# A graph kernel on one Trainium2 core: when the messages are turned, the rows normed, the nodes loaded and the results stored

## The chip, the cores and the metric

One NeuronCore of a Trainium2 chip runs the whole program; nothing is shared with other cores. The metric is the device time of one execution in microseconds (us), lower is better. TensorE is called PE here, its weight loads PEld, VectorE DVE, ScalarE ACT, GpSimd POOL, and SyncE SP. SP computes nothing here: its queue holds DMA issues. ACT issues DMAs too, in order with its own computing instructions.

## What is computed

There are 4096 nodes with 128 features each, and a 4096 x 4096 matrix `adj` (64 MB in fp32).

```python
h = jnp.maximum(_layernorm(x, axis=-1), 0.0)
x = x + _L0_gnn_ref(h, adj)          # (adj.T @ h) / column sums of adj
h = jnp.maximum(_layernorm(x, axis=-1), 0.0)
x = x + _L1_gnn_ref(h, adj, L1_gnn_W, L1_gnn_b)
# inside _L1_gnn_ref
neigh1 = adj @ x
x1 = jax.nn.swish(neigh1 @ W + b)
neigh2 = adj @ x1
x2 = jax.nn.swish(neigh2 @ W + b)
```

So the matrix is passed over three times: once with its columns as outputs (sweep 1), and twice with its rows as outputs (`adj @ x` and `adj @ x1`, sweeps 2 and 3).

## The kernel before, in words

**Two ways to multiply.** PE multiplies a tile of `adj` with a tile of features either whole, in fp32 (each such matmul shows as two MATMUL records), or split: ACT rounds the tile of `adj` to fp32r (`a_hi`, in sweeps 2 and 3 `at_hi`), POOL subtracts that from the original (`a_lo`, `at_lo`), and PE does three cheaper matmuls, hi x hi, hi x lo and lo x hi. A whole one takes more of PE, a split one takes ACT and POOL. Tables (`WHOLE1`, `WHOLE1_FIRST`, `WHOLE3`) say which tiles are whole.

**Sweep 1.** Output columns go in 4 quarters of 1024 columns. In a quarter there are 16 pairs of row tiles, k = 0 to 15; v = 16 * quarter + k counts all 64. Pair v is one 1 MB load by SP into one of 5 slots of `raw1` (`load1`). SP reuses the slot of pair v - 5 when DVE has added that pair to the column sums (`add_degrees`, L559) and PE and POOL are done with it. PE adds the pair into `m_ps`: whole pairs at L277, split pairs at L282 and L283, with the a_lo part (L295) one pair later. In the first quarter pairs 6, 8, 9, 11, 12 and 14 are split, in the others nine of sixteen.

**The start.** `x` is loaded into `h` in three blocks (tiles 0 to 3, 4 to 15, 16 to 31), DVE takes statistics, POOL makes scale and shift (`norm`), and ACT applies them with Relu (L409, one instruction per tile of 128 x 128). For the nine pairs in `SPLIT_ROWS` it does it twice, into `h_hi` and into `h`; POOL then makes `h_lo` of them (L692). ACT goes through all 32 tiles before its first `a_hi`, that of pair 6. Pairs 2, 3 and 5 are whole in the first quarter and split later, so their `h_hi` is first read in the second quarter.

**Messages of a quarter.** When a quarter's 16 pairs are done, ACT copies `m_ps` to `msgT`. While the next quarter runs, PE turns it: after pair k = 2 `turn_message(q, 0)`, the column sums (L322) and four transposes (L330), and after pair k = 6 `turn_message(q, 1)`, the other four transposes, which wait for `inv_ready`. That comes from DVE's `invert` (L571 to L574, after `add_degrees` of k = 7). DVE adds the two halves of the messages to the nodes `x` at k = 8 and k = 11 (`add_message`) and takes statistics at k = 9 and 12 (`node_statistics`). The nodes come in 16 loads of 128 KB each on SP's queue (L252), one after each pair from v = 5 to v = 20; all must be there for the first `add_message`. Each has 1024 runs of 512 bytes.

**Sweeps 2 and 3.** `adj` is loaded again in pieces of 2 MB (`load3`, L217): two DMAs of 512 KB on SP's queue and two on ACT's. Four slots `raw3` hold pieces. DVE transposes each piece in four units (L602) into a ring of five, `turned`. 256 units in 64 pieces are worked off; every third unit is whole (L351) and the others are split (ACT L455, POOL L715, PE L357, L358, L368). Four pieces of sweep 2 are kept for sweep 3. ACT issues its half of piece i between two of its roundings. After 512 rows ACT copies the sums (L463), after 1024 rows PE multiplies by W (`xw`, L376), DVE adds the bias (L612) and ACT applies Silu (L468); in sweep 3 DVE then adds the nodes (L620) and ACT issues the four stores of 128 KB (`store`, L483). There are four such groups in sweep 3, r = 4 to 7, and the last ends the program.

**Order.** There is no scheduler. Each engine's program is written out by hand, and each engine and queue works strictly in its order; semaphores (`wait_ge`) join them.

## Time and profile before

| | us |
|---|---|
| median of 3 runs | 687.6 |
| lowest and highest | 684.11, 690.33 |
| the profiled execution's own time | 688.42 |
| its span, first to last instruction | 686.6 |

| engine | busy us | share of the span |
|---|---|---|
| PE | 634.4 | 92% |
| POOL | 571.2 | 83% |
| DVE | 523.1 | 76% |
| PEld | 404.0 | 59% |
| ACT | 301.4 | 44% |

The DMA engines moved 199.80 MB, 291 GB/s over the span. How to read it: an engine with 92% can still lose time only where it stands idle, and the 52 us in which PE does are spread over a few places. So the places count, not the shares. The profile also gives the granted clock of PE in each stretch, as a share of 2.4 GHz; half of it is 1.2 GHz.

### The profile page before, as it was taken

How to read it: one execution, taken by the hardware profiler on the slowest of the kernel's cores; microseconds unless marked ns; L12 is line 12 of the kernel's file. 1: busy time of each engine (PE TensorE's matmuls, PEld its weight loads, DVE VectorE, ACT ScalarE, POOL GpSimd, SP SyncE). 2: the span in 40 equal slices, each digit the busy share in tenths (PEclk: the TensorE clock that was granted, in tenths of full speed). 3: DMA queues.
4: the chain of work that ended last, by engine and by line, in shares of the span. 5: the costliest groups of instructions: out<-in, count | busy, mean ns of one | idle time of the engine just before them, and what ended most of it. 6: DMA issues, size and time to landing. Idle time of an engine off the chain costs nothing.

```text
span 686.6 us, 6755 instructions
## 1 busy us (share of the span) xinstructions
PE 634.4 (92%) x2212; PEld 404.0 (59%) x2212; DVE 523.1 (76%) x516; ACT 301.4 (44%) x378; POOL 571.2 (83%) x287
## 2 busy tenths in 40 slices
PE   4888978999998988899999999999999999799994
PEld 2355545666665645556666666667666557466553
DVE  3965789979978839777787777878778778577871
ACT  1943243264272343646445445445444434245250
POOL 2288488689788857998999999999999789599693
PEclk9989999999999998999999999999999999899998
DMA  8999996989999899999999999919999999999941
GB/s 277 352 303 306 298 366 246 329 300 333 329 292 309 286 233 250 345 345 317 328 345 330 329 345 317 279 25 195 327 345 345 315 328 332 305 252 347 311 94 31
DMA packets 155762, 199.80 MB, mean 291 GB/s; under 512 B 5456, under 2 KB 138832, under 8 KB 155728
## 3 DMA queue, kind: packets, MB, share of 16 engines
q1 hardware_dynamic: 86672, 133.18, 62.5%
q10 hardware_dynamic: 69056, 66.20, 35.0%
q8 instruction: 17, 0.28, 0.2%
q14 instruction: 17, 0.14, 0.1%
HBM read 197.26 MB, written 2.10 MB: 290 GB/s over the span
## 4 chain that ended last, share of the span: by engine, by line
PE 55%; POOL 20%; issue 12%; DMA 4%; ACT 3%; DVE 3%; ACTq 1%; SPq 1%; POOLq 0%
PE dg L351 20%; POOL a_lo L701 11%; PE dg L368 9%; PE dg L357 9%; PE dg L358 9%; POOL at_lo L715 7%; PE m_ps L277 4%; DMA raw<-in_adj_dram 2%; PE m_ps L376 2%; DMA h<-in_x_dram 2%; POOL norm L684 1%; PE m_ps L295 1%; PE m_ps L282 1%; PE m_ps L283 1%; ACTq L217 1%
## 5 line engine op out<-in xcount | busy, mean ns | idle before, releaser
L715 POOL TENSOR_TENSOR at_lo<-turned,at_hi 128x1024 fp32r<-128x1024 f32 x160 | 379.8, 2414 | 33.1 <-ACT at_hi L455 28.3
L602 DVE STREAM_TRANSPOSE turned<-raw 128x1024 f32<-128x1024 f32 x256 | 304.1, 1224 | 95.7 <-PE dg L351 41.9
L455 ACT ACTIVATE at_hi<-turned 128x1024 fp32r<-128x1024 f32 x160 | 167.3, 1057 | 208.8 <-DVE turned L602 122.2
L701 POOL TENSOR_TENSOR a_lo<-raw,a_hi 128x1024 fp32r<-128x1024 f32 x66 | 155.1, 2387 | 46.7 <-ACT a_hi L425 44.7
L351 PE MATMUL dg<-turned,f_w 128*128 128x512 f32 x384 | 182.4, 597 | 1.3 <-issue 1.3
L559 DVE TENSOR_TENSOR dg<-raw,dg 128x2048 f32<-128x2048 f32 x60 | 137.5, 2291 | 35.5 <-DMA raw<-in_adj_dram 33.6
L357 PE MATMUL dg<-at_hi,f_hi 128*128 128x512 f32 x320 | 134.9, 422 | 11.5 <-ACT at_hi L455 11.5
L368 PE MATMUL dg<-at_lo,f_hi 128*128 128x512 f32 x320 | 130.9, 490 | 3.1 <-POOL at_lo L715 3.1
L358 PE MATMUL dg<-at_hi,f_lo 128*128 128x512 f32 x320 | 128.4, 401 | 0.0
L277 PE MATMUL m_ps<-raw,h 128*128 128x512 f32 x248 | 116.6, 617 | 11.1 <-DMA raw<-in_adj_dram 11.1
L351 PEld LDWEIGHTS dg<-turned,f_w 128*128 128x128 f32 x384 | 73.2, 191 | 57.0 <-issue 48.5
L425 ACT ACTIVATE a_hi<-raw 128x1024 fp32r<-128x1024 f32 x66 | 66.3, 1051 | 91.1 <-DMA raw<-in_adj_dram 86.0
L368 PEld LDWEIGHTS dg<-at_lo,f_hi 128*128 128x128 f32 x320 | 59.6, 192 | 54.3 <-issue 30.4
L277 PEld LDWEIGHTS m_ps<-raw,h 128*128 128x128 f32 x248 | 48.8, 199 | 63.3 <-issue 57.3
L357 PEld LDWEIGHTS dg<-at_hi,f_hi 128*128 128x128 f32 x320 | 61.3, 192 | 32.8 <-ACT at_hi L455 14.3
L358 PEld LDWEIGHTS dg<-at_hi,f_lo 128*128 128x128 f32 x320 | 61.4, 192 | 16.1 <-issue 2.9
L282 PE MATMUL m_ps<-a_hi,h_hi 128*128 128x512 f32 x132 | 55.1, 417 | 6.3 <-ACT a_hi L425 3.8
L283 PE MATMUL m_ps<-a_hi,h_lo 128*128 128x512 f32 x132 | 53.2, 403 | 0.0
L295 PE MATMUL m_ps<-a_lo,h_hi 128*128 128x512 f32 x132 | 46.1, 466 | 0.0
L282 PEld LDWEIGHTS m_ps<-a_hi,h_hi 128*128 128x128 f32 x132 | 25.6, 194 | 16.2 <-issue 8.8
L295 PEld LDWEIGHTS m_ps<-a_lo,h_hi 128*128 128x128 f32 x132 | 25.4, 192 | 15.0 <-issue 9.1
L283 PEld LDWEIGHTS m_ps<-a_hi,h_lo 128*128 128x128 f32 x132 | 25.8, 195 | 5.4 <-issue 0.5
(47 smaller groups left out, 258.8 us busy)
## 6 DMA issues: line engine op xcount, KB each, us to landing
raw<-in_adj_dram SPq DMA_DIRECT2D x64, 1024.0 KB, 8.9
raw<-in_adj_dram ACTq DMA_DIRECT2D x122, 512.0 KB, 13.5
raw<-in_adj_dram SPq DMA_DIRECT2D x118, 512.0 KB, 11.7
x<-in_x_dram SPq DMA_DIRECT2D x16, 128.0 KB, 13.5
out_dram<-zs ACTq DMA_DIRECT2D x16, 128.0 KB, 10.9
h<-in_x_dram SPq DMA_DIRECT2D x1, 768.0 KB, 9.3
h<-in_x_dram SPq DMA_DIRECT2D x1, 256.0 KB, 3.3
w<-in_L_gnn_W_dram ACTq DMA_DIRECT2D x1, 64.0 KB, 3.0
```

The source lines that it names most:

```text
L277: mm = pe.matmul(acc, h[:, 2 * k + i], raw1[:, v % RAW1, i, cols], start=first, stop=False)
L282: pe.matmul(acc, h_hi[:, r], a_hi[:, s % RING1, cols], start=first, stop=False)
L283: mm = pe.matmul(acc, h_lo[:, r], a_hi[:, s % RING1, cols], start=False, stop=False)
L351: mm = pe.matmul(acc, f_w[:, UC * WHOLE3.index(j) + c], turned[:, unit % TURN, c], start=first and c == 0, stop=False)
L357: pe.matmul(acc, f_hi[:, r + c], at_hi[:, s, c], start=first and c == 0, stop=False)
L358: mm = pe.matmul(acc, f_lo[:, r + c], at_hi[:, s, c], start=False, stop=False)
L368: mm = pe.matmul(dg[:, 0, (n % 2) * 512:(n % 2 + 1) * 512], f_hi[:, r + c], at_lo[:, s, c], start=False, stop=unit + 1 == last_unit(n) and ...
L455: act.activation(at_hi[:, s % RING3], turned[:, unit % TURN], ACT.Copy).then_inc(hi3_done, 1)
L559: dve.tensor_tensor(dg[:, :, :], src, dg[:, :, :], ALU.add).then_inc(deg_added, 1)
L602: dve.transpose(dst, src).then_inc(t3_done, 1)
L701: pool.tensor_tensor(a_lo[:, s % RING1], raw1[:, v % RAW1, i], a_hi[:, s % RING1].bitcast(f32), ALU.subtract).then_inc(lo1_done, 1)
L715: pool.tensor_tensor(at_lo[:, s % RING3], turned[:, unit % TURN], at_hi[:, s % RING3].bitcast(f32), ALU.subtract).then_inc(lo3_done, 1)
```

## The change

It has five parts. (1) `turn_message(q, 1)` moves on PE from after pair k = 6 to after pair k = 9, and with it on DVE the second `add_message` from k = 11 to 12 and its statistics from 12 to 13. (2) The node loads go four to a quarter, after pairs k = 3, 6, 9 and 12, each quarter with its own semaphore. (3) ACT norms rows only as far as two pairs beyond the split pair that it is about to round; `h_hi` of pairs 2, 3 and 5 is rounded from `h` just before the second quarter (`round_late`, three instructions of 128 x 256). (4) The stores of groups 4 to 6 go to SP's queue, after loads 47, 55 and 63; SP also takes over the last wait for the stores. (5) The last group (r = 7) is done in two halves of four tiles: PE signals each half, bias, Silu, residual and stores run per half, and the stores of two blocks are issued by SP and of two by ACT.

```diff
@@ -17,8 +17,9 @@
-SPLIT_ROWS = (6, 8, 9, 11, 12, 14, 2, 3, 5)
-NODES_FROM = 5
+LATE_ROWS = (2, 3, 5)
+SPLIT_ROWS = (6, 8, 9, 11, 12, 14) + LATE_ROWS
+NODES_AT = (3, 6, 9, 12)
@@ -41,6 +42,7 @@
+STORE_AT = (47, 55, 63)
@@ -218,6 +221,20 @@
+        def parts(r):
+            return (0, 1) if r == GROUPS - 1 else (0,)
+        def tiles(r, part):
+            n = QT // len(parts(r))
+            return slice(part * n, (part + 1) * n)
+        def store(eng, r, part, blocks):
+            q, m = ORDER[2 * r] // 2, tiles(r, part)
+            eng.wait_ge(y_ready, r - QUARTERS + part + 1)
+            for b in blocks:
+                eng.dma_start(out_nodes[q, b][:, m], zs[b * SB:(b + 1) * SB, r % 2, m]).then_inc(y_out[r % 2], 16)
@@ -247,12 +264,19 @@
-                if NODES_FROM <= v < NODES_FROM + QUARTERS * (P // SB):
-                    q, b = (v - NODES_FROM) // (P // SB), (v - NODES_FROM) % (P // SB)
-                    sp.dma_start(x[b * SB:(b + 1) * SB, q * QT:(q + 1) * QT], x_nodes[q, b]).then_inc(nodes_loaded, 16)
+                if v % PAIRS in NODES_AT:
+                    q, b = v // PAIRS, NODES_AT.index(v % PAIRS)
+                    sp.dma_start(x[b * SB:(b + 1) * SB, q * QT:(q + 1) * QT], x_nodes[q, b])\
+                      .then_inc(nodes_loaded[q], 16)
...
+                if i in STORE_AT:
+                    store(sp, GROUPS // 2 + STORE_AT.index(i), 0, range(P // SB))
+            for part in parts(GROUPS - 1):
+                store(sp, GROUPS - 1, part, SP_BLOCKS)
+            for r in (0, 1):
+                sp.wait_ge(y_out[r], 16 * (P // SB) * sum(len(parts(n)) for n in range(QUARTERS + r, GROUPS, 2)))
@@ -372,17 +396,18 @@
-                for m in range(QT):
-                    mm = pe.matmul(m_ps[:, m * P:(m + 1) * P], nT[:, r % 2, m * P:(m + 1) * P], w[:, :],
-                                   start=True, stop=True)
-                mm.then_inc(xw_done, 1)
+                for part in parts(r):
+                    for m in range(QT)[tiles(r, part)]:
+                        mm = pe.matmul(m_ps[:, m * P:(m + 1) * P], nT[:, r % 2, m * P:(m + 1) * P], w[:, :],
+                                       start=True, stop=True)
+                    mm.then_inc(xw_done, 1)
...
-                if v >= PAIRS and v % PAIRS == 6:
+                if v >= PAIRS and v % PAIRS == 9:
@@ -408,12 +433,21 @@
-            def head(b):
-                act.wait_ge(norm_ready, b + 1)
-                for t in range(*HEAD[b]):
-                    if t // 2 in SPLIT_ROWS:
-                        relu(h_hi[:, 2 * SPLIT_ROWS.index(t // 2) + t % 2], h[:, t], t)
+            def norm_rows(k):
+                for b in range(len(HEAD)):
+                    if HEAD[b][0] == 2 * k:
+                        act.wait_ge(norm_ready, b + 1)
+                for t in (2 * k, 2 * k + 1):
+                    if k in splits1:
+                        relu(h_hi[:, 2 * SPLIT_ROWS.index(k) + t % 2], h[:, t], t)
...
+            def round_late(k):
+                r = 2 * SPLIT_ROWS.index(k)
+                act.wait_ge(h_ready, 2 * k + 2)
+                act.activation(h_hi[:, r:r + 2], h[:, 2 * k:2 * k + 2], ACT.Copy).then_inc(late_rounded, 1)
@@ -463,9 +497,10 @@
-            def silu(r):
-                act.wait_ge(z_ready, r + 1)
-                act.activation(zs[:, r % 2], zs[:, r % 2], ACT.Silu).then_inc(silu_done, 1)
+            def silu(r, part=0):
+                z = zs[:, r % 2, tiles(r, part)]
+                act.wait_ge(z_ready, r + part + 1)
+                act.activation(z, z, ACT.Silu).then_inc(silu_done, 1)
@@ -476,15 +511,15 @@
-            def store(r):
-                q = ORDER[2 * r] // 2
-                act.wait_ge(y_ready, r - QUARTERS + 1)
-                for b in range(P // SB):
-                    act.dma_start(out_nodes[q, b], zs[b * SB:(b + 1) * SB, r % 2]).then_inc(y_out[r % 2], 16)
-            for b in range(len(HEAD)):
-                head(b)
+            normed = 0
...
+                while normed < PAIRS and normed < v + 3:
+                    norm_rows(normed)
+                    normed += 1
+                if v == splits1[split_before(PAIRS)]:
+                    for late in LATE_ROWS:
+                        round_late(late)
@@ -514,14 +549,11 @@
-                ended = group_after(unit, 16)
-                if ended is not None and ended % 2 == 1 and ended >= GROUPS:
-                    store(pair_of(ended))
...
-            silu(GROUPS - 1)
-            store(GROUPS - 1)
-            for r in (0, 1):
-                act.wait_ge(y_out[r], 2 * 16 * (P // SB))
+            for part in parts(GROUPS - 1):
+                silu(GROUPS - 1, part)
+            for part in parts(GROUPS - 1):
+                store(act, GROUPS - 1, part, ACT_BLOCKS)
@@ -576,8 +608,8 @@
-                if q == 0 and part == 0:
-                    dve.wait_ge(nodes_loaded, 16 * QUARTERS * (P // SB))
+                if part == 0:
+                    dve.wait_ge(nodes_loaded[q], 16 * (P // SB))
@@ -601,23 +633,24 @@
-            def add_bias(r):
-                dve.wait_ge(xw_done, r + 1)
+            def add_bias(r, part=0):
+                m = tiles(r, part)
+                dve.wait_ge(xw_done, r + part + 1)
...
-                dve.tensor_tensor(zs[:, r % 2], m_ps[:, :].rearrange("p (t d) -> p t d", d=P),
-                                  bias[:, :].rearrange("p (a d) -> p a d", a=1).to_broadcast([P, QT, P]),
-                                  ALU.add).then_inc(z_ready, 1)
-            def residual(r):
-                q = ORDER[2 * r] // 2
-                y = zs[:, r % 2]
-                dve.wait_ge(silu_done, r + 1)
-                dve.tensor_tensor(y, y, x[:, q * QT:(q + 1) * QT, :], ALU.add).then_inc(y_ready, 1)
+                dve.tensor_tensor(zs[:, r % 2, m], m_ps[:, :].rearrange("p (t d) -> p t d", d=P)[:, m],
+                                  bias[:, :].rearrange("p (a d) -> p a d", a=1)
+                                  .to_broadcast([P, QT // len(parts(r)), P]), ALU.add).then_inc(z_ready, 1)
+            def residual(r, part=0):
+                q, m = ORDER[2 * r] // 2, tiles(r, part)
+                y = zs[:, r % 2, m]
+                dve.wait_ge(silu_done, r + part + 1)
+                dve.tensor_tensor(y, y, x[:, q * QT:(q + 1) * QT][:, m], ALU.add).then_inc(y_ready, 1)
@@ -633,9 +666,9 @@
-                    if k == 11:
+                    if k == 12:
...
-                    if k == 12:
+                    if k == 13:
@@ -660,8 +693,10 @@
-            add_bias(GROUPS - 1)
-            residual(GROUPS - 1)
+            for part in parts(GROUPS - 1):
+                add_bias(GROUPS - 1, part)
+            for part in parts(GROUPS - 1):
+                residual(GROUPS - 1, part)
@@ -689,6 +724,8 @@
+                if k in LATE_ROWS:
+                    pool.wait_ge(late_rounded, LATE_ROWS.index(k) + 1)
@@ -730,8 +767,8 @@
-                if v == splits1[len(SPLIT_ROWS) - 3]:
-                    for late in SPLIT_ROWS[6:]:
+                if v == splits1[split_before(PAIRS)]:
+                    for late in LATE_ROWS:
...
```

ACT's order at the start of the program. The names: `h` and `h_hi` are the normed rows, `a_hi` a rounded half pair of `adj`. Before, the end of the norming and the first roundings:

```order
L409 ACTIVATE h<-h,norm 128x128 x3
L409 ACTIVATE h_hi<-h,norm 128x128
L409 ACTIVATE h<-h,norm 128x128
L409 ACTIVATE h_hi<-h,norm 128x128
L409 ACTIVATE h<-h,norm 128x128 x3
L425 ACTIVATE a_hi<-raw 128x1024 x12
```

Now, from ACT's first computing instruction on:

```order
L434 ACTIVATE h<-h,norm 128x128 x12
L434 ACTIVATE h_hi<-h,norm 128x128
L434 ACTIVATE h<-h,norm 128x128
L434 ACTIVATE h_hi<-h,norm 128x128
L434 ACTIVATE h<-h,norm 128x128 x3
L434 ACTIVATE h_hi<-h,norm 128x128
L434 ACTIVATE h<-h,norm 128x128
L434 ACTIVATE h_hi<-h,norm 128x128
L434 ACTIVATE h<-h,norm 128x128
L459 ACTIVATE a_hi<-raw 128x1024 x2
```

The first rounding of `adj` (two instructions, pair 6) stood behind all Relu instructions; now it stands behind those of pairs 0 to 8.

PE's order in the second quarter around the second half of the turning (`tp<-ident,msgT`). Before:

```order
L282 MATMUL m_ps<-a_hi,h_hi 128x512
L283 MATMUL m_ps<-a_hi,h_lo 128x512
L282 MATMUL m_ps<-a_hi,h_hi 128x512
L283 MATMUL m_ps<-a_hi,h_lo 128x512
L295 MATMUL m_ps<-a_lo,h_hi 128x512 x4
L330 MATMUL tp<-ident,msgT 128x128 x4
L277 MATMUL m_ps<-raw,h 128x512 x4
L295 MATMUL m_ps<-a_lo,h_hi 128x512 x4
```

Now, its new place:

```order
L306 MATMUL m_ps<-a_hi,h_hi 128x512
L307 MATMUL m_ps<-a_hi,h_lo 128x512
L306 MATMUL m_ps<-a_hi,h_hi 128x512
L307 MATMUL m_ps<-a_hi,h_lo 128x512
L319 MATMUL m_ps<-a_lo,h_hi 128x512 x4
L354 MATMUL tp<-ident,msgT 128x128 x4
L301 MATMUL m_ps<-raw,h 128x512 x4
L319 MATMUL m_ps<-a_lo,h_hi 128x512 x4
```

It stood ahead of pair 23, which is whole, and stands now ahead of pair 26, also whole; pairs 23, 24 and 25 have moved ahead of it.

SP's queue at the start (`raw` is a pair of `adj`, `h` and `x` are feature tiles). Before:

```order
L246 DMA h<-in_x_dram 128x4x128
L242 DMA raw<-in_adj_dram 128x2x1024
L246 DMA h<-in_x_dram 128x12x128
L242 DMA raw<-in_adj_dram 128x2x1024
L246 DMA h<-in_x_dram 128x16x128
L242 DMA raw<-in_adj_dram 128x2x1024 x4
L252 DMA x<-in_x_dram 32x8x128
L242 DMA raw<-in_adj_dram 128x2x1024
L252 DMA x<-in_x_dram 32x8x128
L242 DMA raw<-in_adj_dram 128x2x1024
L252 DMA x<-in_x_dram 32x8x128
```

Now:

```order
L263 DMA h<-in_x_dram 128x4x128
L259 DMA raw<-in_adj_dram 128x2x1024
L263 DMA h<-in_x_dram 128x12x128
L259 DMA raw<-in_adj_dram 128x2x1024
L263 DMA h<-in_x_dram 128x16x128
L259 DMA raw<-in_adj_dram 128x2x1024 x2
L269 DMA x<-in_x_dram 32x8x128
L259 DMA raw<-in_adj_dram 128x2x1024 x3
L269 DMA x<-in_x_dram 32x8x128
L259 DMA raw<-in_adj_dram 128x2x1024 x3
L269 DMA x<-in_x_dram 32x8x128
```

The first node load (`x`) has moved ahead of the loads of pairs 4 and 5, and after that one in three loads of a pair has one behind it, where each had.

## Rows read from the trace of the kernel before

**Rows 1.** Windows table: stretch, length, PE, PEld, DVE, ACT, POOL busy, PEclk, DMA, GB/s.

```profile
134.90:187.50 52.60, 51.56 (x190) 33.42 (x189) 48.25 (x46) 23.76 (x32) 45.60 (x23) 1.00 0.91 318
187.50:243.60 56.10, 53.74 (x189) 33.60 (x187) 47.16 (x48) 24.12 (x35) 46.26 (x23) 0.97 0.93 283
...
300.00:530.00 230.00, 230.00 (x846) 152.67 (x845) 180.61 (x152) 113.02 (x123) 223.02 (x103) 1.00 1.02 296
530.00:598.00 68.00, 61.76 (x217) 38.73 (x217) 51.23 (x43) 24.93 (x26) 53.91 (x23) 0.98 1.11 322
```

**Rows 2.** Timeline of PE in sweep 1: start, duration, instruction, count, [idle before <-releaser].

```profile
36.63 0.77 PE L282 MATMUL m_ps<-a_hi,h_hi 128*128 128x512 f32 x1 [2.81 <-ACT a_hi L425]
...
59.16 0.47 PE L282 MATMUL m_ps<-a_hi,h_hi 128*128 128x512 f32 x1 [2.47 <-POOL h_lo L692]
...
81.81 0.47 PE L282 MATMUL m_ps<-a_hi,h_hi 128*128 128x512 f32 x1 [0.66 <-ACT a_hi L425]
...
104.75 1.11 PE L330 MATMUL tp<-ident,msgT 128*128 128x128 f32 x4 [5.75 <-DVE deg L574]
...
105.66 4.52 PE L277 MATMUL m_ps<-raw,h 128*128 128x512 f32 x8
...
115.51 3.59 PE L277 MATMUL m_ps<-raw,h 128*128 128x512 f32 x8
...
158.66 0.66 PE L330 MATMUL tp<-ident,msgT 128*128 128x128 f32 x4 [1.04 <-DVE deg L574]
...
212.51 0.66 PE L330 MATMUL tp<-ident,msgT 128*128 128x128 f32 x4 [2.35 <-DVE deg L574]
...
213.00 5.29 PE L277 MATMUL m_ps<-raw,h 128*128 128x512 f32 x8
```

**Rows 3.** Timeline of ACT, then of POOL, in the first quarter.

```profile
35.44 1.99 ACT L425 ACTIVATE a_hi<-raw 128x1024 fp32r<-128x1024 f32 x2
...
36.56 4.71 POOL L701 TENSOR_TENSOR a_lo<-raw,a_hi 128x1024 fp32r<-128x1024 f32 x2 [10.47 <-ACT a_hi L425]
...
65.61 4.73 POOL L701 TENSOR_TENSOR a_lo<-raw,a_hi 128x1024 fp32r<-128x1024 f32 x2 [1.21 <-ACT a_hi L425]
```

**Rows 4.** Timeline of DVE: column sums that wait for pairs' landings.

```profile
40.63 2.30 DVE L559 TENSOR_TENSOR dg<-raw,dg 128x2048 f32<-128x2048 f32 x1 [1.48 <-DMA raw<-in_adj_dram]
...
44.68 2.30 DVE L559 TENSOR_TENSOR dg<-raw,dg 128x2048 f32<-128x2048 f32 x1 [1.76 <-DMA raw<-in_adj_dram]
...
94.38 2.30 DVE L559 TENSOR_TENSOR dg<-raw,dg 128x2048 f32<-128x2048 f32 x1 [0.24 <-DMA raw<-in_adj_dram]
...
96.94 2.30 DVE L559 TENSOR_TENSOR dg<-raw,dg 128x2048 f32<-128x2048 f32 x1 [0.26 <-DMA raw<-in_adj_dram]
```

**Rows 5.** Timeline of ACT, then of PE, in the fourth quarter (pair 59).

```profile
225.58 2.00 ACT L425 ACTIVATE a_hi<-raw 128x1024 fp32r<-128x1024 f32 x2 [6.23 <-DMA raw<-in_adj_dram]
...
227.96 0.39 PE L282 MATMUL m_ps<-a_hi,h_hi 128*128 128x512 f32 x1
```

**Rows 6.** Timeline of ACT around a store, then of PE behind two stores.

```profile
584.44 6.35 ACTq L483 DMA_DIRECT2D out_dram<-zs  x4
590.84 5.26 ACTq L217 DMA_DIRECT2D raw<-in_adj_dram  x2
596.22 1.06 ACT L455 ACTIVATE at_hi<-turned 128x1024 fp32r<-128x1024 f32 x1 [10.73 <-issue]
...
597.33 0.79 PE L357 MATMUL dg<-at_hi,f_hi 128*128 128x512 f32 x1 [4.40 <-ACT at_hi L455]
...
651.51 0.50 PE L357 MATMUL dg<-at_hi,f_hi 128*128 128x512 f32 x1 [1.50 <-ACT at_hi L455]
```

**Rows 7.** Timeline of DVE in sweep 3, behind the first store.

```profile
559.67 2.37 DVE L602 STREAM_TRANSPOSE turned<-raw 128x1024 f32<-128x1024 f32 x2 [1.45 <-DMA raw<-in_adj_dram]
```

**Rows 8.** Timeline of PE, then of ACT, at the end.

```profile
676.56 2.05 PE L376 MATMUL m_ps<-w,nT 128*128 128x128 f32 x16 [0.73 <-ACT nT L463]
...
682.26 1.89 ACTq L483 DMA_DIRECT2D out_dram<-zs  x4
```

3 lines of the change are left out of this document (2 added, 1 removed).

## The prediction

> **What bounds the kernel now.** I read the windows table first, cut at the quarters of sweep 1 and at the places where PE falls short. From 300 to 530 us PE is busy in 230.00 of 230.00 us; there nothing can be won without taking work from PE, and the change takes none [rows 1]. So every term must be a place where PE stands idle or runs at a low clock. The timeline of PE gives them for sweep 1: 2.81 us at 36.63 and 2.47 at 59.16 in the first quarter, 0.66 at 81.81, and three waits of the second turning for DVE's `deg`, 5.75, 1.04 and 2.35 us [rows 2]. They have a second price. The first whole pair behind the wait of 5.75 takes 4.52 us and the one behind 2.35 takes 5.29, the usual one 3.59 [rows 2]: such a pair is partly worked at 1.2 GHz instead of 2.4, and the granted clock of the fourth quarter is 0.97 where the third has 1.00 [rows 1]. In sweep 3 the stretch from 530 to 598 has 6.24 us without PE, 4.40 of them at one place, and 1.50 follow at 651.51 [rows 1, 6]. Behind PE stand others with little room: DVE is busy 48.25 of 52.60 us in the third quarter, POOL 223.02 of 230, and the DMA share is 1.11 from 530 to 598 [rows 1]. The profiled execution took 688.4 us, 0.8 above the median of 687.6; the sum is made against 688.4, of which 1.8 lies outside the span of 686.6 and stays.
>
> **First quarter (norming ahead, fewer node loads): 4.0 us.** ACT starts its first `a_hi` at 35.44, behind all its Relus, while PE has been free since 33.8 (36.63 less 2.81) and POOL has waited 10.47 us [rows 2, 3]. Of the Relus, 28 of 50 no longer stand in front. Pair 6's landing, which the rows do not show, then starts it; at best it lands early and POOL gains nearly the 2.8 us that PE waited, at worst nothing is won. I take 2.0. POOL is what paces the rest of the quarter: each split pair costs it 4.7 us and an `h_lo`, and the wait at 59.16 is for its `h_lo` [rows 2, 3]. Two small holes remain in it, one of them the 1.21 us at 65.61, where `a_hi` was late because its pair was [rows 3]. Pairs with a node load behind each land 4.05 us apart (40.63 to 44.68), pairs without 2.56 (94.38 to 96.94) [rows 4]. So a node load of 128 KB costs 1.5 us of the queue, and seven fewer before pair 16 free some 10 us of it. That closes both holes: 2.0 more. The late roundings on ACT (three instructions) and POOL's three `h_lo` fall into waits before the second quarter; without that cover they would cost some 3 us. Between nothing and PE's 5.3 us with its slow stretches (some 8) I take 4.0.
>
> Here a page differs from the rows. The Trainium skill, in "DMA: Bandwidth & Descriptors", section "Specifications", gives line rate for runs from 512 bytes up, and about 358 GB/s for a core's share of the memory; a node load would by that, as an estimate, cost 0.4 us. The trace has 1.5 and does not agree. By the page POOL's holes would stay and the sum be 2 us smaller.
>
> **Second quarter: 7.8 us.** The wait of 5.75 goes, since PE now has pairs 23, 24 and 25 to do first, 8.9 us of work (115.51 less 105.66, less the 0.93 of the slow pair), more than each of the three waits. With it goes the slow stretch, 0.45 at the turning itself (1.11 against 0.66) and 0.93 at the pair behind it (4.52 against 3.59) [rows 2]. The 0.66 before pair 18 goes because that pair, with nine fewer node loads ahead of it, lands before PE wants it. 5.75 + 1.38 + 0.66 = 7.8. DVE has the second message only one pair later, while the turning comes three pairs later on PE. DVE is the one ahead (it adds pair 23 at 96.94, PE would turn behind pair 22 at 99.0), so part of its room goes; I take what is left to be enough. If it isn't, DVE waits with the following pairs' sums queued behind, and their slots of `raw1` come free later [rows 2, 4].
>
> **Third quarter: 1.0 us.** The wait of 1.04 goes. Four node loads come in, 6 us of the queue. With 318 GB/s and a share of 0.91 there is room for them, and slots run ahead [rows 1]; I charge nothing. At the other end they cost 6.
>
> **Fourth quarter: a loss of 1.7 us.** The wait of 2.35 and the slow pair behind it (5.29 - 3.59 = 1.70) are 4.05 us. But landings are next in line. Here SP's loads share the DMA engines with the first piece of sweep 2. `a_hi` of pair 59 starts at 225.58, at its landing, its first half is there 1.1 us later, and PE takes it at 227.96 [rows 5]: 1.3 us of room, so 1.3 of the 4.05 can be had. Two new node loads stand before that landing and cost 1.5 each [rows 4]. 1.3 - 3.0 = -1.7. The bounds are +4.05 and -6.
>
> **Stores on SP's queue: 7.3 us.** ACT issues four DMAs of a store for 6.35 us and two of a piece for 5.26, and only then rounds the next unit, after 10.73 us; PE waits 4.40 and then has half the clock for a while: its first matmul takes 0.79, and the eight of that unit take 2.0 us more with what follows [rows 6]. That is 6.4. The first store has the rest of the 6.24 idle us, 1.84 (its waits are of one kind with these), and the third 1.50 [rows 1, 6]. Together 9.8. Without stores ACT only issues the pieces, as elsewhere in the sweep, where PE does not wait. What stays is the transfer: a store is four DMAs like the node loads, with the same runs, so 4 x 1.5 = 6 us of a queue [rows 4]. DVE waited 1.45 us for a landing behind the first store, so there is little room [rows 7]. I charge 2.5 for the first two stores together; the third comes behind the last load on SP and delays only ACT's half. 9.8 - 2.5 = 7.3. Bounds: 9.8, and 2 if each of two stores costs PE half of its 6 us, with a slow clock behind it.
>
> **The end in halves: 2.4 us.** Behind the last matmul (676.56 + 2.05 = 678.6) come bias, Silu and residual, one after the other until ACT's issue at 682.26; the four issues take 1.89, and the span ends 2.45 later [rows 8]. In halves the first half starts 1.0 earlier and the second follows in a pipeline: an estimate from 678.6 is three steps of 0.65, then two issues on each of two queues behind those of the first half, the last over at 681.7. 684.15 - 681.7 = 2.4. It is 1 if half instructions cost nearly whole ones.
>
> **Sum.** 4.0 + 7.8 + 1.0 - 1.7 + 7.3 + 2.4 = 20.8, and 688.4 - 20.8 = 667.6. I predict 667.5 us.
>
> **Rivals.**
> - *Loads set the pace of sweep 1.* What the turning gives back is then waited for at landings. For it: DMA shares of 0.91 and 0.93, and the landing of pair 59 [rows 1, 5]. Against: no pair of the third quarter made PE wait. Without 7.1 of the second quarter, with 1 us lost in the third: about 676.
> - *The stores' transfers were the cost, not their issue.* Then the term of 7.3 becomes 2: 673. For it: the share of 1.11 and the wait for a landing behind the first store [rows 1, 7]. Against: ACT's 10.73 us stand as "issue" and not as a landing. The Trainium skill ("Trainium Kernel Development and Optimization", section "Key Constraints") says that the queues of SP and ACT share the same 16 DMA engines, and that another issuing engine saves issue time alone; the trace's issue of 6.35 us is that time.
> - *Landings have more room than I give them.* The fourth quarter gives its 4.05 and the stores are not charged: 688.4 - 29.0 = 659.4.
> - *Node loads stop PE (slower).* The eight of the third and fourth quarters each make PE wait 1.5 us, and behind each it runs slowly, 1.5 to 3 us more. 8 x 4.0 = 32 against the 22.5 of the other terms (without the -1.7): 698. It decides from about six of the eight on. Against: a single one needs room of under 1.5 us, which only the fourth quarter shows.
>
> **How the numbers follow.** My forecast has 0.52 (663 to 671), the loads 0.15, the transfers 0.14, more room 0.12, the slower case 0.03, and 0.04 goes to the first two together, about 681. 660 to 677 leaves out the last two and a piece of the third: it holds 8 in 10. About 1% (6.9 us) is what a measurement of this kernel can tell from no change. Faster: 0.93. Within 1%: 0.04. Slower: 0.03.
>
> **What would show it.** Right: PE enters the third quarter at about 123 us instead of 134.9 and the fourth at about 175 instead of 187.5; no wait for `deg` at a turning; in the fourth quarter `a_hi` waits for landings and PE for `a_hi`; no ACT wait of 10 us at L455 in sweep 3; 7.6 us from the start of the last PE group to the end of the span, where it is 10.0 now. Wrong: waits of PE for `raw` or `a_hi` in the second or third quarter, a DVE wait at the second message, or DVE waits for landings of 3 us and more behind the stores.

## The result, and the profile after

| | before | changed |
|---|---|---|
| median of 4 runs, us | 687.13 | 663.28 |
| lowest and highest, us | 684.11, 690.33 | 661.49, 675.77 |
| the profiled execution's own time, us | 688.42 | 661.49 |
| its span, us | 686.6 | 659.7 |
| PE busy, us | 634.4 | 626.2 |
| mean granted clock | 0.971 | 0.989 |

The ratio of the times is 0.9639, with a 95% interval of 0.9586 to 0.9691: some 24 us, or 3.6%, less. (The 675.77 is from a slow run; it counts in the median and not in the ratio.) The prediction was 667.5 us with a range of 660 to 677. The two profiled executions differ by 26.9 us.

The page of the changed kernel, part 1 (busy us, share of the span, instructions):

```profile
PE 626.2 (95%) x2212; PEld 401.7 (61%) x2212; DVE 520.9 (79%) x518; ACT 302.0 (46%) x376; POOL 571.3 (87%) x287
```

PE does the same matmuls in 8.2 us less of busy time, since fewer of them run at half the clock (mean granted clock 0.989 against 0.971); the rest of the gain is waits. Where it lies is read best from marks that both profiles have: PE's first turning matmul of a quarter of sweep 1 (L322 before, L346 after) and the first matmul by `w` of a group (L376, L401). This table is worked out from the starts of those rows, in us:

| stage, to the mark | before | changed | gain | predicted |
|---|---|---|---|---|
| start to the turning of quarter 1 | 84.16 | 77.53 | 6.6 | 4.7 |
| to that of quarter 2 | 59.45 | 51.29 | 8.2 | 7.1 |
| to that of quarter 3 | 52.55 | 51.29 | 1.3 | 1.0 |
| quarter 4 and sweep 2, to `w` of group 0 | 120.69 | 122.28 | -1.6 | -1.7 |
| groups 0 to 4 | 201.09 | 201.08 | 0 | 0 |
| groups 4 to 5, 5 to 6, 6 to 7 | 53.41, 57.07, 48.15 | 50.08, 53.41, 45.28 | 9.9 | 7.3 |
| `w` of group 7 to the end | 10.07 | 7.45 | 2.6 | 2.4 |

(The predicted 0.66 before pair 18 lies in the first stage by these marks.) The windows table of the changed kernel, cut at the quarters and in sweep 3; columns as in [rows 1]:

```profile
77.50:128.80 51.30, 51.30 (x189) 33.52 (x188) 46.55 (x46) 23.12 (x32) 42.56 (x23) 1.00 0.97 338
128.80:180.10 51.30, 51.30 (x189) 33.52 (x188) 49.92 (x47) 23.76 (x34) 45.32 (x23) 1.00 0.98 338
180.10:240.00 59.90, 53.16 (x194) 33.93 (x192) 42.09 (x47) 23.56 (x34) 44.36 (x23) 0.94 0.96 256
300.00:515.00 215.00, 215.00 (x796) 143.65 (x795) 168.33 (x142) 105.96 (x116) 208.31 (x97) 1.00 1.01 293
515.00:582.00 67.00, 67.00 (x245) 44.67 (x244) 56.35 (x48) 31.41 (x31) 63.50 (x27) 1.00 1.10 336
```

The second and third quarters are now full: PE is busy in every microsecond, at a clock of 1.00. With this work on PE and at this clock a quarter cannot be shorter than 51.3. The fourth is short of it, with 6.7 us idle and a clock of 0.94. The stretch 515 to 582, in which the first store now goes out, is full too; the like stretch of before was 6.24 us short [rows 1].

What PE waits for in the whole changed kernel, the largest (engine, line, releaser, us in total, times, longest; the 8.6 us that PE waits at the very start, as before, are left out):

```profile
PE m_ps L306 <- ACT a_hi L459: 6.0, 7, 2.2
PE dg L381 <- ACT at_hi L489: 4.0, 3, 3.5
PE m_ps L306 <- POOL h_lo L729: 2.4, 1, 2.4
```

No wait for `deg` is left, where there were three [rows 2]. The timeline of PE in the changed kernel has the new turning, the two waits of the fourth quarter and the one wait of 1.9 in sweep 3 that follows the stores:

```profile
44.72 0.51 PE L306 MATMUL m_ps<-a_hi,h_hi 128*128 128x512 f32 x1 [2.40 <-POOL h_lo L729]
...
100.27 0.60 PE L354 MATMUL tp<-ident,msgT 128*128 128x128 f32 x4
...
204.04 0.47 PE L306 MATMUL m_ps<-a_hi,h_hi 128*128 128x512 f32 x1 [2.19 <-ACT a_hi L459]
...
218.85 0.56 PE L306 MATMUL m_ps<-a_hi,h_hi 128*128 128x512 f32 x1 [2.18 <-ACT a_hi L459]
...
599.46 1.95 PE L375 MATMUL dg<-turned,f_w 128*128 128x512 f32 x4 [1.87 <-DVE turned L634]
```

The timeline of ACT in the changed kernel says what the fourth quarter waits for, and it is the landings, as was said of pair 59 in [rows 5]:

```profile
202.84 2.00 ACT L459 ACTIVATE a_hi<-raw 128x1024 fp32r<-128x1024 f32 x2 [2.69 <-DMA raw<-in_adj_dram]
```

### The profile page after: what moved, and what is told of

Its sections match the earlier page's. It is cut to its first block, busy times and chain, and to the rows that moved or that the text cites. A ratio compares the mean times of both kernels' runs of the same rounds, so it can differ in the third digit from the quotient of the medians.

```text
span 659.7 us, 6763 instructions
## 1 busy us (share of the span) xinstructions
PE 626.2 (95%) x2212; PEld 401.7 (61%) x2212; DVE 520.9 (79%) x518; ACT 302.0 (46%) x376; POOL 571.3 (87%) x287
## 4 chain that ended last, share of the span: by engine, by line
PE 60%; POOL 21%; issue 11%; DMA 3%; DVE 2%; ACT 1%; SPq 1%; ACTq 0%; POOLq 0%; DVEq 0%
PE dg L375 22%; POOL a_lo L738 14%; PE dg L392 10%; PE dg L381 10%; PE dg L382 10%; POOL at_lo L752 6%; PE m_ps L301 3%; PE m_ps L401 2%; DMA h<-in_x_dram 2%; DMA raw<-in_adj_dram 1%; DVE dg L591 1%; PE m_ps L306 1%; POOL norm L719 1%; PE m_ps L307 1%; PE m_ps L319 1%
## 5 line engine op out<-in xcount | busy, mean ns | idle before, releaser
L381 PE MATMUL dg<-at_hi,f_hi 128*128 128x512 f32 x320 | 133.2, 416 | 4.1 <-ACT at_hi L489 4.0
L382 PE MATMUL dg<-at_hi,f_lo 128*128 128x512 f32 x320 | 126.4, 395 | 0.0
L301 PE MATMUL m_ps<-raw,h 128*128 128x512 f32 x248 | 114.0, 606 | 10.0 <-ACT h L434 8.6
L459 ACT ACTIVATE a_hi<-raw 128x1024 fp32r<-128x1024 f32 x66 | 66.1, 1050 | 79.9 <-DMA raw<-in_adj_dram 79.3
L301 PEld LDWEIGHTS m_ps<-raw,h 128*128 128x128 f32 x248 | 47.8, 194 | 60.3 <-issue 55.5
L306 PEld LDWEIGHTS m_ps<-a_hi,h_hi 128*128 128x128 f32 x132 | 25.8, 195 | 19.4 <-issue 11.6
## 6 DMA issues: line engine op xcount, KB each, us to landing
x<-in_x_dram SPq DMA_DIRECT2D x16, 128.0 KB, 7.5
out_dram<-zs SPq DMA_DIRECT2D x12, 128.0 KB, 12.6
```

Of the source, the lines that this page charges most:

```text
L301: mm = pe.matmul(acc, h[:, 2 * k + i], raw1[:, v % RAW1, i, cols], start=first, stop=False)
L306: pe.matmul(acc, h_hi[:, r], a_hi[:, s % RING1, cols], start=first, stop=False)
L381: pe.matmul(acc, f_hi[:, r + c], at_hi[:, s, c], start=first and c == 0, stop=False)
L382: mm = pe.matmul(acc, f_lo[:, r + c], at_hi[:, s, c], start=False, stop=False)
```

## The experiments

In each kernel whose name begins with `a_` one thing is altered in the changed kernel (in a_wide two, in a_wide_piece three), in each with `b_` one thing in the kernel before. Whole times of most of these kernels scatter by 2 to 9 us, more than most parts are worth. So the stages are compared, between the same marks as above. They agree to 0.1 us wherever PE is full. Elsewhere they scatter too, and each is from one profiled execution. How much can be read off kernels that have the same code in a stage: the first stage of the changed kernel takes 77.5 to 78.4 us (six kernels), its part from the fourth quarter to group 0 takes 119.8 to 122.9 (five kernels), its three stretches from group 4 to 7 together 148.1 to 152.3 (six kernels). In the kernel before, with b_stores_none, which has the same code up to group 4, the second quarter takes 59.5 and 61.9 and the part from the fourth quarter on 120.7 and 117.3.

| kernel | to turning 1 | 2 | 3 | to `w` of 0 | 4 to 5, 5 to 6, 6 to 7 | tail | span | ratio to before, 95% |
|---|---|---|---|---|---|---|---|---|
| before | 84.2 | 59.5 | 52.6 | 120.7 | 53.4, 57.1, 48.2 | 10.1 | 686.6 | |
| changed | 77.5 | 51.3 | 51.3 | 122.3 | 50.1, 53.4, 45.3 | 7.5 | 659.7 | 0.964 [0.959, 0.969] |
| a_turn6 | 78.3 | 51.3 | 56.6 | 122.7 | 50.1, 52.7, 45.3 | 7.3 | 665.5 | 0.964 [0.957, 0.972] |
| a_nodes_old | 87.1 | 55.4 | 51.3 | 116.8 | 50.1, 54.3, 45.1 | 7.4 | 668.4 | 0.970 [0.964, 0.976] |
| a_norm_old | 80.8 | 51.3 | 51.3 | 122.7 | 50.1, 56.1, 46.1 | 7.3 | 666.8 | 0.965 [0.960, 0.970] |
| a_end_whole | 77.6 | 51.3 | 51.3 | 122.9 | 50.1, 53.3, 45.2 | 9.7 | 662.4 | 0.966 [0.960, 0.971] |
| a_stores_act | 78.0 | 51.3 | 51.3 | 121.1 | 54.0, 56.8, 48.5 | 7.3 | 669.4 | 0.977 [0.970, 0.984] |
| a_stores_none | 78.4 | 51.3 | 51.3 | 119.8 | 50.1, 50.1, 44.8 | 7.2 | 654.0 | 0.955 [0.948, 0.962] |
| b_stores_none | 84.2 | 61.9 | 52.5 | 117.3 | 50.1, 50.1, 44.8 | 10.0 | 671.9 | 0.980 [0.973, 0.987] |
| b_nodes_long | 84.5 | 60.3 | 52.6 | 120.1 | 53.1, 56.5, 47.6 | 10.1 | 685.7 | 1.000 [0.996, 1.005] |
| b_nodes_wide | 89.4 | 61.3 | 52.5 | 122.3 | 54.4, 54.5, 46.9 | 10.1 | 692.4 | 1.013 [1.002, 1.024] |
| a_wide | 79.3 | 51.3 | 51.3 | 128.0 | 65.8, 68.6, 44.8 | 7.3 | 697.4 | 1.012 [1.004, 1.020] |
| a_wide_piece | 79.5 | 58.2 | 58.2 | 117.5 | 65.8, 68.8, 44.8 | 7.4 | 701.2 | 1.018 [1.011, 1.024] |
| a_piece_spread | 78.2 | 51.3 | 53.6 | 118.2 | 50.1, 56.0, 45.0 | 7.4 | 660.8 | 0.962 [0.956, 0.969] |

Groups 0 to 4 took 201.1 in all of them.

### The turning back after pair k = 6

```diff
-                if v >= PAIRS and v % PAIRS == 9:
+                if v >= PAIRS and v % PAIRS == 6:
```

with `add_message(q, 1)` back at k = 11 and its statistics at 12.

> The changed kernel with the second half of the turning back behind pair k = 6 (DVE's message and statistics back at k = 11 and 12); all else stays. Theory (the turning is worth its waits for deg with their slow clock, where nothing else waits): waits of some 5, 1 and 1 us at L354 come back in quarters 2 to 4; the second and third quarters lose 6 to 8 us together, but the fourth, where landings pace PE, loses nothing, since a wait for deg there takes the place of a wait for a landing. End result 668 to 671 us. Rival (loads set the pace of sweep 1, the turning's wait was hidden behind them): 662 to 664 us, as the changed kernel. Second rival (the freed queue alone shortened invert's lateness, so the wait is gone without the move): no wait at L354, 662 to 664 us; the trace tells it from the first by showing no wait for landings either.

The timeline of PE in a_turn6 at the turnings in quarters 2, 3 and 4:

```profile
92.19 0.60 PE L354 MATMUL tp<-ident,msgT 128*128 128x128 f32 x4
...
147.01 0.66 PE L354 MATMUL tp<-ident,msgT 128*128 128x128 f32 x4 [3.37 <-DVE deg L606]
147.51 5.29 PE L301 MATMUL m_ps<-raw,h 128*128 128x512 f32 x8
...
202.76 1.11 PE L354 MATMUL tp<-ident,msgT 128*128 128x128 f32 x4 [2.51 <-DVE deg L606]
```

In the second quarter `deg` is there in time here even at k = 6, and the stage is 51.29 with either place. It would be rash to conclude that the earlier landings alone took the 5.75 us away [rows 2]. The last three instructions of `invert`, each on a tile of 128 x 8, say why. Timeline of DVE in a_turn6, then of POOL there:

```profile
90.89 0.28 DVE L604 TENSOR_SCALAR deg<-deg 128x8 f32<-128x8 f32 x1
91.20 0.17 DVE L605 TENSOR_TENSOR deg<-deg 128x8 f32<-128x8 f32 x1
91.41 0.17 DVE L606 TENSOR_TENSOR deg<-deg 128x8 f32<-128x8 f32 x1
...
86.39 4.75 POOL L738 TENSOR_TENSOR a_lo<-raw,a_hi 128x1024 fp32r<-128x1024 f32 x2
92.14 4.71 POOL L738 TENSOR_TENSOR a_lo<-raw,a_hi 128x1024 fp32r<-128x1024 f32 x2 [0.99 <-ACT a_hi L459]
```

The same of the changed kernel, and PE's pair 23, which starts when pair 22 (k = 6) is done:

```profile
88.37 1.54 DVE L604 TENSOR_SCALAR deg<-deg 128x8 f32<-128x8 f32 x1
89.94 2.31 DVE L605 TENSOR_TENSOR deg<-deg 128x8 f32<-128x8 f32 x1
92.28 2.28 DVE L606 TENSOR_TENSOR deg<-deg 128x8 f32<-128x8 f32 x1
...
82.80 18.78 POOL L738 TENSOR_TENSOR a_lo<-raw,a_hi 128x1024 fp32r<-128x1024 f32 x8 [0.42 <-PE m_ps L319]
...
91.38 3.59 PE L301 MATMUL m_ps<-raw,h 128*128 128x512 f32 x8
```

In a_turn6 POOL happened to be idle for 0.99 us, and the three took 0.6 us together. In the changed kernel POOL subtracts without a pause, and they took 6.1: `deg` is ready at 94.56, but PE is through with pair 22 at 91.38. A turning at k = 6 would have waited 3.2 us in that execution (an estimate from these rows, as is the next figure). a_end_whole, a_stores_act and a_stores_none, which have the same code here, have gaps of 3.2 to 3.6 us between the same two events. Only a_piece_spread has none; there POOL was idle behind the first of the three. So the earlier landings took away about 2.5 of the 5.75 us, and the move the rest, but for executions such as the one of a_turn6.

In the third quarter PE arrives at the turning 14 us earlier than before (143.6, where it was 157.6). `deg` is ready only 11.6 us earlier (the three instructions take 7.1 us there), and the wait grows from 1.04 to 3.37, with a slow pair behind (5.29 where 3.59 is usual). There the move is worth 5.3 us in the profiled execution. The whole times do not show it: the ratio of 0.964 is that of the changed kernel, and one execution of a_turn6 took 660.76 us, less than the fastest of the changed kernel (661.49). What the move is worth on average is therefore not shown. In the fourth quarter the stage (122.7) is no longer than in kernels that have the move: 2.51 is waited at the turning, and less at landings.

### The node loads back to one behind each of pairs 5 to 20

```diff
-                if v % PAIRS in NODES_AT:
-                    q, b = v // PAIRS, NODES_AT.index(v % PAIRS)
+                if 5 <= v < 5 + QUARTERS * (P // SB):
+                    q, b = (v - 5) // (P // SB), (v - 5) % (P // SB)
```

> The changed kernel with the sixteen node loads back behind pairs 5 to 20, one each (the semaphores per quarter stay). Theory (a node load takes 1.5 us of the queue wherever landings pace PE): pairs of the first quarter land 4.05 us apart again, POOL gets the two holes back, the second quarter starts 3 to 4 us later than 70, and PE may wait for landings or deg in the second quarter, 3 to 6 us more; against that the fourth quarter, free of its four node loads, gives back 4 to 6 us. Net 664 to 668 us. Rival (node loads cost by the page's line rate, 0.4 us each): within 2 us of the changed kernel in every quarter.

The first quarter is 9.5 us longer, the second 4.1, and the part from the fourth quarter to group 0 is 5.4 shorter: spreading them gives 8.2 us net between the two profiled executions (with the scatter given above, 8.7 to 9.5 in the first and 3.0 to 6.1 in the last). By the whole times it is some 4 us (0.970 against 0.964), with intervals of 4 us on either side. With the norming ahead and the node loads as before, the first quarter is 2.9 us longer than in the kernel before. The timeline of PE in a_nodes_old:

```profile
47.89 0.68 PE L306 MATMUL m_ps<-a_hi,h_hi 128*128 128x512 f32 x1 [2.93 <-POOL h_lo L729]
...
60.18 0.47 PE L306 MATMUL m_ps<-a_hi,h_hi 128*128 128x512 f32 x1 [1.56 <-POOL h_lo L729]
...
84.00 0.47 PE L306 MATMUL m_ps<-a_hi,h_hi 128*128 128x512 f32 x1 [1.53 <-ACT a_hi L459]
```

The windows table of this kernel has its second quarter without a single idle microsecond of PE, at a granted clock of 0.92:

```profile
87.05:142.42 55.37, 55.37 (x189) 37.02 (x188) 51.19 (x48) 25.20 (x34) 46.32 (x24) 0.92 0.93 330
```

So with the node loads as before the turning at k = 9 has no wait for `deg` either, and what the quarter still loses is the slow clock behind the wait at 84.00.

The parts depend on each other: the norming ahead is no gain of its own. It gives 3.2 us where the loads are early (next run) and, by this comparison, costs 2.9 where they are late.

### All rows normed first

```diff
-                while normed < PAIRS and normed < v + 3:
+                while normed < PAIRS:
```

> The changed kernel with all rows normed before ACT's first a_hi (pairs 2, 3 and 5 are still rounded late). Theory (the start of POOL's chain sets the first quarter's end): the first a_hi starts at about 33 to 34 instead of 32.4, POOL's chain 1 to 1.5 us later, and the whole is later by that, 663 to 665 us: most of the early start would then come from the six Relus that are gone (2.3 us), not from the interleaving. Rival (the interleaving itself is what helped): 2.5 us or more later, 666 us.

The first stage is 80.8 instead of 77.5, 3.2 us more (2.4 against the longest of the kernels with the same code here). PE, which in the changed kernel takes pair 6 without a wait, has one again (timeline of PE, a_norm_old):

```profile
37.12 0.47 PE L306 MATMUL m_ps<-a_hi,h_hi 128*128 128x512 f32 x1 [2.53 <-ACT a_hi L459]
```

All other stages up to group 0 agree within 0.5. The expectation of 1 to 1.5 us was too low, and its rival, that the interleaving itself helps, is the nearer one. I don't put the longer groups 5 to 7 (56.1 and 46.1) down to the edit: in the six kernels with the same four-part stores on SP and the same code there, groups 5 to 6 came out between 52.7 and 56.1.

### The last group whole

```diff
-            return (0, 1) if r == GROUPS - 1 else (0,)
+            return (0,)
```

> The changed kernel with the last group in one piece again (its stores two by SP and two by ACT). Theory (the halves overlap and shorten the tail from xw's start to the end by 2.6 us): of these about 0.9 come from splitting the four issues between two queues, which this kernel keeps; so the tail is 9.1 us instead of 7.4 and the whole 1.7 us slower, about 664.5. Rival (all of the gain is the two queues' issues): no difference, 662 to 663.

The tail is 9.65 us. Timeline of DVE, ACT and SP at the end, first of the changed kernel, then of a_end_whole:

```profile
653.45 0.69 DVE L645 TENSOR_TENSOR zs<-m_ps,bias 128x512 f32<-128x512 f32 x1 [8.46 <-PE m_ps L401]
654.17 0.63 ACT L503 ACTIVATE zs<-zs 128x512 f32<-128x512 f32 x1 [1.98 <-DVE zs L645]
655.66 1.78 SPq L236 DMA_DIRECT2D out_dram<-zs  x4
655.66 1.88 ACTq L236 DMA_DIRECT2D out_dram<-zs  x4
```

```profile
654.80 1.23 DVE L645 TENSOR_TENSOR zs<-m_ps,bias 128x1024 f32<-128x1024 f32 x1 [9.32 <-PE m_ps L401]
656.06 1.06 ACT L503 ACTIVATE zs<-zs 128x1024 f32<-128x1024 f32 x1 [3.40 <-DVE zs L645]
658.40 0.81 SPq L236 DMA_DIRECT2D out_dram<-zs  x2
```

The halves cost 0.69 and 0.63 where the whole costs 1.23 and 1.06, so they pipeline. They give 2.2 of the 2.6 us; the four issues divided over two queues give the other 0.4, less than the 0.9 that was expected of them.

### Stores on ACT again, and no stores in either kernel

```diff
-                if i in STORE_AT:
-                    store(sp, GROUPS // 2 + STORE_AT.index(i), 0, range(P // SB))
...
+                ended = group_after(unit, 16)
+                if ended is not None and ended % 2 == 1 and ended >= GROUPS:
+                    store(act, pair_of(ended), 0, range(P // SB))
```

> The changed kernel with the stores of groups 4 to 6 back on ACT's queue; the end in halves stays. Theory (ACT's blocked queue was the cost): from the fifth xw (group 4) to the last it takes 157 to 159 us again instead of 148.7, with an ACT wait of about 10 us at L489 marked issue and PE waits of some 4.4 and 1.5 us; the whole is 671 to 673 us. Rival (transfers were the cost, the queue does not matter; what the changed kernel gained in sweep 3 came from sweep 1's earlier landings): the stretch stays within 2 us of 148.7.

The other two only drop the stores of groups 4 to 6, the first in the changed kernel:

```diff
-                if i in STORE_AT:
-                    store(sp, GROUPS // 2 + STORE_AT.index(i), 0, range(P // SB))
```

> The changed kernel without the stores of groups 4 to 6: these twelve DMAs and the waits for them are left out, so three quarters of the output are not written. Theory (a store still costs its transfer where landings pace PE, about 2.5 us for the first two together): from the fifth xw to the last 145 to 147 us instead of 148.7, PE's wait of 1.87 us near 599 gone. Rival (the transfers are hidden on SP's queue): 148.5 to 149.

the second in the kernel before:

```diff
-                ended = group_after(unit, 16)
-                if ended is not None and ended % 2 == 1 and ended >= GROUPS:
-                    store(pair_of(ended))
```

> The kernel before without the stores of groups 4 to 6 (twelve DMAs and their waits left out, so three quarters of the output are not written). Together with the run above it divides the price of the stores. Theory: from the fifth xw to the last it takes as long as in the changed kernel without them (145 to 147 us, 158.7 with them); so the stores cost the kernel before 12 to 13 us, of which the move to SP saved 10 and left about 2.5. The whole 675 to 677 us. Rival (the stretch before is long for another reason too, such as landings that come late after sweep 2): 149 us or more stay.

Without these stores both kernels take exactly 50.08, 50.08 and 44.76 us for the three stretches, 144.9 in all. So the stores cost 13.7 us before, 14.4 in a_stores_act and 3.8 in the changed kernel (3.2 to 7.4 in the six kernels with the same stores on SP). The move gives 9.9 us between the two profiled executions, the largest single part, and it shows in the whole times too: 0.977 for a_stores_act against 0.964 is 9 us. Where the 13.7 lay, by the windows table of the kernel before, cut at the same marks:

```profile
517.94:571.34 53.40, 51.56 (x185) 32.68 (x184) 41.58 (x34) 20.50 (x22) 46.28 (x20) 1.00 1.10 327
571.34:628.42 57.08, 52.68 (x186) 34.94 (x185) 41.98 (x36) 24.40 (x25) 49.83 (x22) 0.94 1.11 305
628.42:676.56 48.14, 45.56 (x165) 28.49 (x163) 32.49 (x26) 18.00 (x19) 40.68 (x17) 1.00 0.71 193
```

Only the second of the three stretches has a slow clock. In the first and third PE stands idle for 1.84 and 2.58 us (0.73 of these before `w`, which the kernels without stores have too), and it is busy 1.5 us longer than the 50.08 and 44.03 of b_stores_none, at a clock of 1.00. What makes it busy longer there isn't accounted for. Timeline of ACT in a_stores_act, then of SP in the changed kernel:

```profile
569.80 6.39 ACTq L236 DMA_DIRECT2D out_dram<-zs  x4
576.23 5.74 ACTq L220 DMA_DIRECT2D raw<-in_adj_dram  x2
582.09 1.06 ACT L487 ACTIVATE at_hi<-turned 128x1024 fp32r<-128x1024 f32 x1 [11.24 <-issue]
```

```profile
572.44 6.39 SPq L236 DMA_DIRECT2D out_dram<-zs  x4
```

The four issues of this store take 6.39 us on either engine; those of the other two take 3.3 and 5.6 on ACT and 6.0 and 9.1 on SP. ACT has rounding to do behind them, SP only has loads that are wanted later. What remains shows in the timeline of DVE in the changed kernel, behind the second store:

```profile
598.07 4.62 DVE L634 STREAM_TRANSPOSE turned<-raw 128x1024 f32<-128x1024 f32 x4 [6.14 <-DMA raw<-in_adj_dram]
```

This is the transfer, or the loads held back behind it: 3.3 us in the stretch of groups 5 to 6 and 0.5 behind. The first store costs nothing. That wait of 6.14 us is over the 3 us which the prediction named as a sign of being wrong.

### What a node load costs the queue

The prediction took 1.5 us for 128 KB, and the theory of the first run below puts it down to 512-byte runs. (A node load has 256 of these, 128 KB in all, and not the 1024 of the description of the kernel and of that theory; a quarter's four loads have 1024.) Two kernels alter the form of these loads in the kernel before. One loads as many bytes of other data in runs of 4 KB:

```diff
-                    sp.dma_start(x[b * SB:(b + 1) * SB, q * QT:(q + 1) * QT], x_nodes[q, b]).then_inc(nodes_loaded, 16)
+                    sp.dma_start(x[b * SB:(b + 1) * SB, q * QT:(q + 1) * QT], adj[32 * (4 * q + b):32 * (4 * q + b) + 32, 0:QC].rearrange("p (m d) -> p m d", d=P)).then_inc(nodes_loaded, 16)
```

> The kernel before with its sixteen node loads of the same 128 KB, issued at the same places, but read in runs of 4 KB from the first rows of the matrix instead of 512 bytes (the nodes are then other data, so the output is another). It measures the disputed price of a node load. Theory (1.5 us each is the price of 1024 short runs): pairs of the first quarter land 2.9 us apart instead of 4.05, the second quarter starts 3 to 4 us earlier, and PE's wait for deg at the second quarter's turning shrinks from 5.75 to under 2: 679 to 683 us. Rival (the price is that of any further DMA in the queue, whatever its runs): pairs still land 4 us apart, 687 to 689 us.

The other splits each into two of 64 KB over all 128 partitions:

```diff
+                    for m in (2 * b, 2 * b + 1):
+                        sp.dma_start(x[:, q * QT + m], x_nodes[q, :, :, m]).then_inc(nodes_loaded, 16)
```

> The kernel before with each node load of 128 KB to 32 partitions issued as two of 64 KB to all 128 partitions, at the same places and with the same runs of 512 bytes; the result is the same. The run with long runs has shown that the length of a run is not what a node load costs. Theory (its price comes from going to 32 partitions, a quarter of them): pairs of the first quarter land 2.9 to 3.1 us apart instead of 4.05, the second quarter's first turning comes at about 80 instead of 84.2, and PE's wait for deg in the second quarter shrinks from 5.75 to under 2. Rival (any further DMA in SP's queue costs 0.7 us or more): pairs land 4.05 us apart or, with two DMAs each, further.

Timeline of DVE, whose column sums wait for the landings of pairs with a node load behind each: b_nodes_long, b_nodes_wide, and the changed kernel, which has one such load in this stretch:

```profile
40.61 2.30 DVE L559 TENSOR_TENSOR dg<-raw,dg 128x2048 f32<-128x2048 f32 x1 [1.59 <-DMA raw<-in_adj_dram]
44.66 2.30 DVE L559 TENSOR_TENSOR dg<-raw,dg 128x2048 f32<-128x2048 f32 x1 [1.75 <-DMA raw<-in_adj_dram]
```

```profile
42.13 2.30 DVE L560 TENSOR_TENSOR dg<-raw,dg 128x2048 f32<-128x2048 f32 x1 [2.19 <-DMA raw<-in_adj_dram]
46.51 2.30 DVE L560 TENSOR_TENSOR dg<-raw,dg 128x2048 f32<-128x2048 f32 x1 [2.08 <-DMA raw<-in_adj_dram]
```

```profile
47.12 2.30 DVE L591 TENSOR_TENSOR dg<-raw,dg 128x2048 f32<-128x2048 f32 x1 [0.26 <-DMA raw<-in_adj_dram]
51.13 2.30 DVE L591 TENSOR_TENSOR dg<-raw,dg 128x2048 f32<-128x2048 f32 x1 [1.71 <-DMA raw<-in_adj_dram]
54.26 2.30 DVE L591 TENSOR_TENSOR dg<-raw,dg 128x2048 f32<-128x2048 f32 x1 [0.83 <-DMA raw<-in_adj_dram]
56.80 2.30 DVE L591 TENSOR_TENSOR dg<-raw,dg 128x2048 f32<-128x2048 f32 x1 [0.24 <-DMA raw<-in_adj_dram]
```

The pairs are 4.05 apart with long runs, as with short ones [rows 4], and 4.38 with two DMAs over all partitions. In the changed kernel they are 2.5 to 3.1 apart, and 4.01 at the one place with a node load. The next distance there is longer as well, 3.13 against 2.54, so that a single load costs some 2.0 us. So the 1.5 us stands as a lower figure (1.8 for two DMAs with the same bytes), but my reason for it was wrong: neither the runs nor the 32 partitions alone make it. The bytes alone would take 0.4 us at the 338 GB/s of the windows table. It isn't a fixed price for each DMA either, since two cost only 0.3 more than one. What makes it stays open.

### Wide node loads and stores in the changed kernel

```diff
+                for m in range(QT):
+                    sp.dma_start(out_nodes[q, :, :, m], zs[:, r % 2, m]).then_inc(y_out[r % 2], 16)
```

for the four stores by blocks, and the node loads as in b_nodes_wide. a_wide_piece also loads piece 0 of sweep 2 in four parts, after pairs 22, 28, 38 and 44, and a_piece_spread does only that:

```diff
-                if v // PAIRS == QUARTERS - 1 and v % PAIRS == 6:
-                    load3(act, 0, SP_BLOCKS + ACT_BLOCKS)
+                if v in (22, 28, 38, 44):
+                    load3(act, 0, ((22, 28, 38, 44).index(v),))
```

> The changed kernel with node loads and the stores of groups 4 to 6 going to and from all 128 partitions, 64 KB each (two for a node load, eight for a store). Theory (32 partitions cost the queue 1.5 us per 128 KB, 128 partitions 0.4): from the third quarter's end to the first xw (180 to 302 us) 4 to 5 us less, and in sweep 3, from the fifth xw to the last, 145 to 146 instead of 148.7; together 653 to 656 us. Rival (the price is per DMA, or SP's issuing is the limit): no faster than the changed kernel, 662 to 668.

> As the run before, and the first piece of sweep 2 is loaded by one DMA each after pairs 22, 28, 38 and 44 instead of four after pair 54. Theory (the fourth quarter is paced by landings because this piece shares it): PE has no wait for a_hi in the fourth quarter; the time from its first turning to the first xw falls by 4 to 6 us against the run before, while the second and third quarters have room for it; 648 to 652 us. Rival (all of sweep 1 is at the limit of its DMAs, so the piece costs there what it saves): within 2 us of the run before.

> The changed kernel with only the first piece of sweep 2 spread over the second and third quarters (after pairs 22, 28, 38 and 44), loads and stores as they are. Theory: PE's waits for a_hi in the fourth quarter (2.2 us twice and smaller ones) go, the stretch from 180 us to the first xw falls from 122.3 to 117 or 118, 657 to 659 us in all. Rival (no room in the second and third quarters): these grow by as much, 662 to 665.

Eight DMAs over 128 partitions in place of four over 32 made the stores much worse: 15.7 and 15.2 us more in the two stretches with a store that has loads behind it. The timeline of SP, then of PE, in a_wide:

```profile
526.72 19.02 SPq L254 DMA_DIRECT2D out_dram<-zs  x8
...
567.78 3.75 PE L381 MATMUL dg<-turned,f_w 128*128 128x512 f32 x4 [12.79 <-DVE turned L640]
```

SP issues in order, so its piece loads stand behind 19 us of issues, and what they bring comes 12.8 us late. With four DMAs it was 6.0 to 6.4 us, and that fitted into the lead that the loads have. Number and form of the DMAs changed together, so that it isn't shown which of them made each issue longer (2.4 us where it was 1.6). The wide node loads did not help either: to `w` of group 0 the kernel took 128.0 us, with a PE wait of 5.56 us for a landing at 215.43. This is the limit of the move to SP: it costs little as long as SP's queue is ahead by more than the stores take to issue.

Spreading piece 0 shortened the part from the fourth quarter to group 0 by 4.0 us and lengthened the third by 2.3; its span (660.8) and its times (median 662.95) are those of the changed kernel. With the wide node loads as well, quarters 2 and 3 were 58.2 each. The second quarter of a_piece_spread took its two parts for nothing (51.3). The third had PE idle for only 0.23 us in all, but its granted clock was 0.84 from 129.46 to 140.00, and this slow stretch is most of the 2.3. So the quarters have little room for more loads, and none for these together with the wide node loads; that they have none at all isn't shown.

## Why the prediction was right, and where its steps were not

- **What bounds the kernel.** That every term must be a place where PE idles or runs slowly held. The full stages did not move by 0.1 us (201.1 for groups 0 to 4 in every kernel).
- **First quarter: 4.7 predicted, 6.6 measured.** The norming was taken at 2.0 and gives 2.4 to 3.2. The loads were taken at 2.0 plus the 0.66. They pay more and not apart from the norming: put back, they cost 8.7 to 9.5. PE still waits 2.40 at 44.72 for POOL's `h_lo`, so POOL paces this quarter as was said.
- **Second quarter: 7.1 predicted, 8.2 measured** (10.6 against b_stores_none, which has the code of the kernel before there). "The wait of 5.75 goes, since PE now has pairs 23, 24 and 25 to do first" holds: with the node loads as before the wait is gone as well (a_nodes_old), and in the changed kernel `deg` came 3.2 us after PE was through with k = 6. It leaves out two things. The earlier landings shorten the wait too, since DVE's column sums stand before `deg`. And most of the wait was no column sum: pair 23 is added at 99.2 in the kernel before, and the four small instructions of `invert` end only at 104.7, at the end of one of POOL's subtractions. The prediction took DVE's lateness as it stood and did not ask what made it.
- **Third quarter: 1.0 predicted, 1.3 measured.** Here the move, priced at 1.0, was worth 5.3 in the profiled execution, because without it the quarter would have become longer than before. The node loads cost nothing here, as charged.
- **Fourth quarter: -1.7 predicted, -1.6 measured.** `a_hi` waits for landings, as predicted. The two terms of it, 1.3 gained and 3.0 charged, can't be told from the runs. With the node loads out of quarters 3 and 4 the part is 116.8 us: 3.9 less than the kernel before, but only 0.4 less than b_stores_none, which has the code of the kernel before in this part; and 3.0 to 6.1 less than the kernels with node loads. Those came out between 119.8 and 122.9, so the agreement to 0.1 is luck, and even the sign of the whole term hangs on which executions are compared.
- **Stores: 7.3 predicted, 9.9 measured.** The gross was taken at 9.8 and is 13.7: I summed the idle places (1.84, 4.40, 1.50) and 2.0 of slow clock behind one. The stage holds 3.3, 7.0 and 3.4. The slow clock was rightly counted for one of three, since the other two stretches have 1.00. The mistake is to take a wait for its idle time alone: the first and the third store cost 3.3 and 3.4 us where 1.84 and 1.50 were counted. The transfers, charged with 2.5, cost 3.8. The rival that they are the whole cost fell. The Trainium skill ("Trainium Kernel Development and Optimization", section "Key Constraints") has another issuing engine save issue time alone; the runs agree: 9.9 of 13.7 us went with the issuing engine, 3.8 stayed.
- **The end: 2.4 predicted, 2.6 measured**, 2.2 from the halves and 0.4 from the second queue.
- **The sum** was 20.8 and is 26.9 between the two profiled executions. The missing 6 us are 1.9 in the first quarter, 1.1 in the second, 2.6 in the stores and 0.6 elsewhere, all of one sign; the largest is what the waits of the stores cost beyond their idle time. The medians lie only 24 us apart, so 3 us of the 6 are no more than the scatter of single executions.
- **Rivals.** Loads that set the pace of sweep 1 did not come true in quarters 2 and 3, which are full; they do pace the fourth. Node loads that stop PE did not show in the third quarter; in the fourth they cost 3.0 to 6.1. "More room" was near in time (659.4), but not in cause: the stores do cost transfers, and the fourth quarter shows no gain of 4.05.
- **The signs.** Those for being right came, the quarters even earlier than said: PE's mark of the third quarter went from 143.61 to 128.82, 14.8 us, where 11.9 was forecast for the quarter's start. Of those for being wrong one came, the DVE wait for a landing behind a store (6.14 us); it is part of the 3.8 us that the stores still cost.
- **The page on line rate.** The prediction set the 1.5 us against the Trainium skill ("DMA: Bandwidth & Descriptors", section "Specifications"), which gives line rate from 512 bytes up. The runs agree with the page that run length above that size does not matter (4 KB costs what 512 bytes cost), and not with the 0.4 us worked out from it: the price of 1.5 us is real.

No version that writes the whole result beat the changed kernel by more than the scatter. Whether it helps to take only the fourth quarter's node loads forward, to make stores and node loads fewer and larger, or to put `invert` where POOL is idle, was not run.

## What to carry to other kernels

Price each part of a change against the profile as the other parts will leave it: here one move gave most where it was priced least, in the third quarter. Where an engine waits for a small result, look at the instructions that make it and at what runs beside them; a chain of 128 x 8 instructions that takes 0.6 us in one place and 6.1 in another isn't short of landings. Stores belong on the queue of an engine that has nothing to compute behind them, as long as that queue is ahead of its loads by more than they take to issue. A wait can cost more than its idle time, here 3.3 us where 1.84 were idle, even at the full clock. Compare stages between marks rather than whole times when parts are worth a few us each, and take the scatter of a stage from kernels that have the same code in it before you read a difference of 1 to 4 us.

## What the runs showed of the hardware

- **Small DVE instructions are held up while POOL subtracts.** `invert` has three instructions on tiles of 128 x 8 for each turning, 168 of them in the fourteen profiles. Of these 47 took 0.17 to 0.28 us. The other 121 took longer, up to 2.5 us, and every one of them ended within 0.03 us of the end of one of POOL's subtractions of 128 x 1024 (2.4 us each), as at 89.90, 92.25 and 94.56 in the changed kernel. No run altered POOL's work there, so this rests on the times alone.
- **Issuing a DMA takes longer in mid-sweep.** Four stores of 128 KB held their engine for 3.1 to 9.1 us there, on ACT as well as on SP (6.39 for the same one on either), and for 1.89 at the end of the kernel before [rows 8], where nothing else is under way. Eight of 64 KB over 128 partitions took 19.02 us.
- **A small load between large ones costs far more than its bytes.** 128 KB put 1.5 us between pairs of 1 MB, with runs of 512 bytes or of 4 KB alike, where the bytes alone are 0.4 at 338 GB/s.
- **The clock.** Waits of 2.40 and 2.19 us were followed by matmuls of 0.63 us in place of 0.39, which is 1.2 GHz in place of 2.4, and one of 3.37 by matmuls of 1.06 in place of 0.59. Of the shorter ones, those of 0.86 and 1.56 us were not followed by such a stretch, and one of 1.53 (at 84.00 in a_nodes_old) was. In a_piece_spread the clock fell at 133 with no wait above 0.2 us just before it.
